# Preparation of the gated delta rule: TensorE convolves two of four batches, inverse lengths laid out by place in the block, the small solve ordered by source column, picks of k issued first

## The reference, cut to what matters

```python
xn = _rmsnorm(x, norm1_w)
xc = silu(_causal_depthwise_conv(xn, conv_w, conv_b))     # K = 4 taps per channel, causal
q = _l2norm((xc @ wq).reshape(b, t, H, HD))               # 16 heads of 8
k = _l2norm((xc @ wk).reshape(b, t, H, HD))
v = (xc @ wv).reshape(b, t, H, HD)
beta = sigmoid(xc @ wb)
alpha = sigmoid(xc @ wa + 4.0)
def step(S, inp):                                         # one token
    q_, k_, v_, b_, a_ = inp
    S = a_[..., None, None] * S
    pred = einsum('bhkv,bhk->bhv', S, k_)
    S = S + k_[..., :, None] * (b_[..., None] * (v_ - pred))[..., None, :]
    return (S, einsum('bhkv,bhk->bhv', S, q_))
```

## Time and profile before

| what | value |
|---|---|
| median of 3 runs | 1909.59 us (1905.56 to 1911.18) |
| the profiled execution, whole | 1912.84 us |
| its span, first to last instruction | 1911.0 us |
| granted TensorE clock, mean | 0.944 |

### The profile page before, as it was taken

The page is one execution under the profiler, slowest core; times in us unless marked ns, Lnnn a source line. Parts: engine busy times, 40 slices in busy tenths (PEclk is TensorE's granted clock), DMA queues, the critical chain, the costliest instruction groups (busy, mean ns, idle before and its releaser), DMA issues.

```text
span 1911.0 us, 24918 instructions
## 1 busy us (share of the span) xinstructions
PE 1671.2 (87%) x8058; PEld 740.8 (39%) x8058; DVE 1307.9 (68%) x3081; ACT 954.3 (50%) x2056; POOL 297.9 (16%) x460
## 2 busy tenths in 40 slices
PE   6789999999999989999799678445897899979998
PEld 2245545544544432222244221222433454534443
DVE  7477767767767767887564689999566777733333
ACT  2555655646645516676434447333244465653333
POOL 0000000000001022111278000000000222104443
PEclk9999999999999989999999889677798899989999
DMA  4000000000000120230000000000100433000000
GB/s 186 1 1 1 1 1 1 1 1 1 1 1 23 50 75 18 59 110 2 1 0 0 1 0 1 1 1 1 66 0 25 122 74 74 3 1 1 1 0 22
DMA packets 19807, 44.37 MB, mean 23 GB/s; under 512 B 3872, under 2 KB 13024, under 8 KB 18912
## 3 DMA queue, kind: packets, MB, share of 16 engines
q1 hardware_dynamic: 19200, 42.39, 7.4%
q10 hardware_dynamic: 480, 0.39, 0.1%
HBM read 32.74 MB, written 9.44 MB: 22 GB/s over the span
## 4 chain that ended last, share of the span: by engine, by line
PE 72%; DVE 18%; ACT 5%; issue 4%; DMA 1%; POOL 0%; ACTq 0%; POOLq 0%; SPq 0%; DVEq 0%
PE ps L569 8%; PE ps L535 7%; PE ps L547 6%; PE ps L1018 5%; PE ps L1056 5%; PE ps L968 5%; PE ps L504 4%; PE ps L1462 3%; PE ps L1463 3%; PE ps L1351 3%; PE ps L1362 3%; PE ps L1470 3%; DVE arena L1801 2%; PE ps L524 2%; PE ps L578 2%
## 5 line engine op out<-in xcount | busy, mean ns | idle before, releaser
L1173 DVE TENSOR_REDUCE stat<-ps 128x1 f32<-128x512 f32 (+3 forms) x512 | 278.7, 582 | 84.6 <-PE ps L968 41.3
L1104 ACT ACTIVATE arena<-ps 128x512 f32<-128x512 f32 (+3 forms) x512 | 246.3, 515 | 150.1 <-PE ps L1056 81.7
L681 ACT ACTIVATE arena<-ps,stat 128x544 f32<-128x544 f32 x256 | 180.4, 709 | 226.0 <-DVE stat L723 226.0
L723 DVE TENSOR_REDUCE stat<-ps 128x1 f32<-128x544 f32 x256 | 173.6, 720 | 144.8 <-PE ps L535 144.0
L1056 PE MATMUL ps<-arena 75*128 75x512 bf16 (+1 forms) x480 | 163.0, 344 | 9.7 <-ACT arena L1104 7.4
L968 PE MATMUL ps<-arena 72*128 72x128 bf16 (+1 forms) x480 | 163.0, 348 | 8.1 <-DVE stat L1173 7.9
L569 PE MATMUL ps<-arena 128*64 128x512 f32 (+1 forms) x640 | 159.7, 611 | 6.3 <-DVE arena L743 5.5
L535 PE MATMUL ps<-arena 64*128 64x272 f32 x1024 | 153.1, 417 | 12.1 <-ACT arena L681 10.4
L689 ACT COPY arena<-ps 128x512 f32<-128x512 f32 x256 | 137.2, 593 | 16.7 <-PE ps L547 16.7
L547 PEld LDWEIGHTS ps<-wA_sb,arena 128*128 128x128 f32 x1024 | 115.1, 142 | 68.7 <-issue 67.9
L547 PE MATMUL ps<-wA_sb,arena 128*128 128x128 f32 x1024 | 140.0, 280 | 0.0
(11 more groups left out here) (352 smaller groups left out, 2822.3 us busy)
## 6 DMA issues: line engine op xcount, KB each, us to landing
arena<-b_parts SPq DMA_DIRECT2D x180, 96.0 KB
b_parts<-arena SPq DMA_DIRECT2D x64, 128.0 KB, 1.8
reg<-wM_dram SPq DMA_DIRECT2D x1, 3072.0 KB, 9.9
reg<-wB_dram SPq DMA_DIRECT2D x1, 2048.0 KB, 12.7
reg<-wM_dram SPq DMA_DIRECT2D x1, 2048.0 KB, 16.7
reg<-wD_dram SPq DMA_DIRECT2D x1, 1817.0 KB, 10.1
wF_sb<-wF_dram SPq DMA_DIRECT2D x1, 1476.0 KB, 19.9
reg<-b_parts SPq DMA_DIRECT2D x12, 96.0 KB
```

Of the source, the lines that this page charges most:

```text
L681: e.activation(prob_of(P, r).rearrange("p (a k) -> p a k", a=2), score_banks(r), ACT.Exp, bias=x_neg[:, at_:at_ + 1], accum_out=x_sums[:, ...
L723: e.tensor_reduce(x_neg[:, n % 4:n % 4 + 1], score_banks(r), AX.XY, ALU.max, negate=True).then_inc(sem("max_done"), 1)
L1104: e.activation(p_t[:, m % 8, q0:T], ps[:, S1 + m % S2, q0:T], ACT.Exp).then_inc(exp_done, 1)
L1173: e.tensor_reduce(nm[:, G % 2, u // 4, u % 4:u % 4 + 1], ps[:, step % S1, 0:keys(u)], AX.X, ALU.max, negate=True).then_inc(max_done, 1)
```

## The change

Four things are rewritten, all in the preparation:

1. Batches 0 and 1 are convolved by TensorE, as four products each with diagonal matrices (`conv_diag`) that add up in banks 4 and 5; Silu reads the bank. POOL makes the four matrices and the zero columns. DVE convolves batches 2 and 3 only. Projections with `g_wa` start batch by batch, and alpha is made batch by batch.
2. The inverse lengths are written by place (`split_i(r)`), so that DVE reads them in planes.
3. The solve goes by source column: one multiply and one subtract take place j out of all later places at once (3, 2 and 1 planes). The six dots go to banks 0 to 5 in the order that this needs, and the solve waits for all of them.
4. `g_ke` is made right behind `g_k`. Gamma and five picks of `g_ke` are issued ahead of the dots, three behind them. `g_pq[0]` is made ahead of the solve and not behind it.

In the diff below the renaming of three semaphores of the first layer (to `padded`, `convolved`, `diag_made`) is left out.

```diff
...
             g_alpha, g_beta = hist_flat[:, 0:BL * M], hist_flat[:, BL * M:2 * BL * M]
-            g_z, g_tmp = terms_flat[:, 0:BL * M], terms_flat[:, BL * M:BL * M + M]
+            g_z, g_tmp = terms_flat[:, 0:BL * M], terms_flat[:, BL * M:BL * M + 3 * M]
             g_pk, k_sq = y_flat[:, 0:6 * M], y_flat[:, 6 * M:10 * M]
...
             r_k, r_q = g_q, qk[:, 0:B * T]
+            conv_diag = qk[:, 9 * M:10 * M].rearrange("p (k n) -> p k n", k=CTAPS)
+            assert CTAPS * D == M
             g_w, g_u, g_ke = (reg2[:, a * B * T:(a + 1) * B * T] for a in range(3))
...
             PK0 = (None, 0, 3, 5)
+            DOT0 = (0, 3, 5)
+            PEB = 2
+            KE_FIRST = 5
             GAMMA, KE, WW, UU, QK, GQ = 0, 1, 9, 17, 21, 31
             PICKS = 39
-            READY = {x: n_ + 1 for n_, x in enumerate(("gamma", "ke", "gq", "w", "u", "q0", "q1", "q2", "q3"))}
+            READY = {x: n_ + 1 for n_, x in enumerate(("gamma", "ke", "gq", "q0", "w", "u", "q1", "q2", "q3"))}
+
+            def by_m(x, n_):
+                return x[:, 0:n_ * M].rearrange("p (i m) -> p i m", i=n_)
 
...
                 e.wait_ge(sem("load_wD"), 16)
-                e.wait_ge(sem("b4_xc"), 1)
+                e.wait_ge(sem("diag_made"), TAPS + CTAPS)
+                e.wait_ge(sem("padded"), 2)
 
...
                     e.matmul(ps[:, bank, :], wt[w], x_aux[:, b, :], start=True, stop=True).then_inc(sem("b4_proj"), 1)
+                for b in range(PEB):
+                    e.wait_ge(*n4.done(b))
+                    for k in range(CTAPS):
+                        i = e.matmul(ps[:, 4 + b, :], conv_diag[:, k, :], xp[:, b, k:k + T], start=(k == 0),
+                                     stop=(k == CTAPS - 1))
+                    i.then_inc(sem("convolved"), 1)
                 for b in range(B):
+                    e.wait_ge(sem("b4_xc"), min(b, PEB) + 1)
                     proj("g_wa", b, b)
...
                              stop=True).then_inc(sem("b4_sum"), 1)
-                e.wait_ge(sem("b4_dve_read"), 2)
-                e.wait_ge(sem("b4_ln"), 2 * B)
-                for s_ in range(1, BL):
-                    e.wait_ge(sem("b4_prod"), s_)
-                    for x in range(PK0[s_], PK0[s_] + BL - s_):
-                        e.matmul(ps[:, x, :], wt["head_one"], g_pk[:, x * M:x * M + M], start=True,
-                                 stop=True).then_inc(sem("b4_dot"), 1)
-
                 def pick(g, matrix, source):
...
                 e.wait_ge(sem("b4_ready"), READY["ke"])
+                e.wait_ge(sem("b4_ln"), 2 * B)
                 pick(GAMMA, pick_k[0], lambda b: split_i(g_gamma)[:, BL - 1, b, :])
                 for d in range(HD):
+                    if d == KE_FIRST:
+                        e.wait_ge(sem("b4_dve_read"), 2)
+                        for s_ in range(1, BL):
+                            e.wait_ge(sem("b4_prod"), s_)
+                            for j in range(BL - s_):
+                                x = PK0[s_] + j
+                                e.matmul(ps[:, DOT0[j] + s_ - 1, :], wt["head_one"], g_pk[:, x * M:x * M + M],
+                                         start=True, stop=True).then_inc(sem("b4_dot"), 1)
                     pick(KE + d, pick_k[d], whole(g_ke))
...
             def b4_act(e):
+                for b in range(PEB):
+                    e.wait_ge(sem("convolved"), PB + b + 1)
+                    e.activation(x_aux[:, b, :], ps[:, 4 + b, :], ACT.Silu, bias=v("conv_b")).then_inc(sem("b4_xc"), 1)
                 e.wait_ge(sem("b4_conv"), CTAPS)
-                e.activation(x_aux[:, :, :], x_aux[:, :, :], ACT.Silu, bias=v("conv_b")).then_inc(sem("b4_xc"), 1)
-                e.wait_ge(sem("b4_proj"), B)
-                e.activation(split_i(g_alpha), tokens_by_i(ps[:, 0:B, :]), ACT.Sigmoid,
-                             bias=v("four")).then_inc(sem("b4_act_read"), 1)
+                e.activation(x_aux[:, PEB:, :], x_aux[:, PEB:, :], ACT.Silu, bias=v("conv_b")).then_inc(sem("b4_xc"), 1)
+                for b in range(B):
+                    e.wait_ge(sem("b4_proj"), b + 1)
+                    i = e.activation(split_i(g_alpha)[:, :, b, :], tokens_by_i(ps[:, b:b + 1, :])[:, :, 0, :], ACT.Sigmoid,
+                                     bias=v("four"))
+                i.then_inc(sem("b4_act_read"), 1)
                 e.wait_ge(sem("b4_proj"), 2 * B)
...
                     for b in range(B):
-                        x, done = r[:, b * T:b * T + T], n_ * B + b + 1
+                        x, done = split_i(r)[:, :, b, :], n_ * B + b + 1
                         e.wait_ge(sem("b4_sum"), done)
-                        e.activation(x, ps[:, 4 + b, :], ACT.Ln, bias=v("eps6")).then_inc(sem("b4_ln"), 1)
+                        e.activation(x, tokens_by_i(ps[:, 4 + b:5 + b, :])[:, :, 0, :], ACT.Ln,
+                                     bias=v("eps6")).then_inc(sem("b4_ln"), 1)
                         e.wait_ge(sem("b4_ln"), done)
...
             def b4_dve(e):
-                link(e, e.memset(xp[:, :, 0:PADW], 0.0))
-                for b in range(B):
+                e.wait_ge(sem("padded"), 2)
+                for b in range(PEB, B):
                     e.wait_ge(*n4.done(b))
+                own = x_aux[:, PEB:, :]
                 for k in range(CTAPS):
                     if k == 0:
-                        i = e.tensor_scalar(x_aux[:, :, :], xp[:, :, 0:T], v("conv_w"), None, ALU.mult)
+                        i = e.tensor_scalar(own, xp[:, PEB:, 0:T], v("conv_w"), None, ALU.mult)
                     else:
                         e.wait_ge(sem("b4_conv"), k)
-                        i = e.scalar_tensor_tensor(out=x_aux[:, :, :], in0=xp[:, :, k:k + T], scalar=v("conv_w", k),
-                                                   in1=x_aux[:, :, :], op0=ALU.mult, op1=ALU.add)
+                        i = e.scalar_tensor_tensor(out=own, in0=xp[:, PEB:, k:k + T], scalar=v("conv_w", k),
+                                                   in1=own, op0=ALU.mult, op1=ALU.add)
                     i.then_inc(sem("b4_conv"), 1)
...
                     e.tensor_tensor(split_i(g_k)[:, :, b, :], tokens_by_i(ps[:, b:b + 1, :])[:, :, 0, :],
-                                    tokens_by_i(r_k[:, b * T:b * T + T].unsqueeze(1))[:, :, 0, :],
-                                    ALU.mult).then_inc(sem("b4_khat"), 1)
+                                    split_i(r_k)[:, :, b, :], ALU.mult).then_inc(sem("b4_khat"), 1)
+                e.wait_ge(sem("b4_khat"), B)
+                e.wait_ge(sem("b4_ready"), READY["gamma"])
+                e.tensor_tensor(g_ke, g_k, g_to_end, ALU.mult).then_inc(sem("b4_ready"), 1)
                 e.wait_ge(sem("b4_act_read"), 2)
-                e.wait_ge(sem("b4_khat"), B)
                 link(e, e.tensor_tensor(g_z, g_k, g_beta, ALU.mult))
...
                 e.tensor_tensor(split_i(g_q), tokens_by_i(ps[:, 0:B, :]),
-                                tokens_by_i(r_q.rearrange("p (b t) -> p b t", b=B)), ALU.mult).then_inc(sem("b4_dve_read"), 1)
-                e.tensor_tensor(g_ke, g_k, g_to_end, ALU.mult).then_inc(sem("b4_ready"), 1)
+                                split_i(r_q), ALU.mult).then_inc(sem("b4_dve_read"), 1)
                 e.wait_ge(sem("b4_dve_read"), 2)
+                e.wait_ge(sem("b4_ready"), READY["ke"])
                 e.tensor_tensor(g_gq, g_q, g_gamma, ALU.mult).then_inc(sem("b4_ready"), 1)
+                e.tensor_tensor(g_pq[0], g_q, g_k, ALU.mult).then_inc(sem("b4_ready"), 1)
                 e.wait_ge(sem("b4_prod"), BL - 1)
+                e.wait_ge(sem("b4_dot"), len(DOT0) * (len(DOT0) + 1) // 2)
                 for x in (g_w, g_u):
                     x_ = by_i(x)
-                    for i in range(1, BL):
-                        for s_ in range(1, i + 1):
-                            pair = PK0[s_] + i - s_
-                            e.wait_ge(sem("b4_dot"), pair + 1)
-                            link(e, e.tensor_tensor(g_tmp, ps[:, pair, :], x_[:, i - s_, :], ALU.mult))
-                            o = e.tensor_tensor(x_[:, i, :], x_[:, i, :], g_tmp, ALU.subtract)
-                            if i == s_ == BL - 1:
-                                o.then_inc(sem("b4_ready"), 1)
-                                e.wait_ge(sem("b4_ready"), READY["w" if x is g_w else "u"])
-                            else:
-                                link(e, o)
-                for s_ in range(BL):
+                    for j in range(BL - 1):
+                        n_ = BL - 1 - j
+                        link(e, e.tensor_tensor(by_m(g_tmp, n_), ps[:, DOT0[j]:DOT0[j] + n_, :],
+                                                x_[:, j, :].unsqueeze(1).to_broadcast([128, n_, M]), ALU.mult))
+                        o = e.tensor_tensor(x_[:, j + 1:, :], x_[:, j + 1:, :], by_m(g_tmp, n_), ALU.subtract)
+                        if n_ == 1:
+                            o.then_inc(sem("b4_ready"), 1)
```

(31 more changed lines are left out.)

## The result

The changed kernel has a median of 1901.17 us over 8 runs (1892.79 to 1910.70), the kernel before 1909.98 beside it; the ratio is 0.9953, 95% interval 0.9930 to 0.9976. So it is faster by 0.5%, some 9 us. The forecast was 1900.1 and faster by over 0.3%.

A forecast was written before the change was run, and what follows sets the result against it. Two strands, picks on TensorE and ACT and DVE's work, end together before the scan, so both must shorten. Terms sum to -11.0 us, less 1.5 for the clock: 9.5 us less, median 1900.1, range 1895 to 1905.

The forecast's parts named there:

- Convolution, -7.75: From the last norm product to beta: with TensorE convolving two batches, beta starts 7.75 us earlier, partly through clock.
- Lengths by place, -0.4 and -1.45: Scaling of k and q on DVE: SBUF operand in planes saves 0.4 us on k's last batch, 1.45 on q.
- the SBUF rival: Scaling of k and q: SBUF steps are free, PSUM's cost, so 7.65 us less, 1901.9; chance 0.04.
- `g_ke` forward, +2.3, and dots, +1.0: On DVE, `g_ke` ahead of `g_z` adds 2.3 us; waiting for six dots starts the solve 1.0 later behind `g_q`.
- Solve, -2.35: DVE's solve by source column: 15.05 us instead of 17.4, so 2.35 less.
- The rival rate of `g_q`: Solve's multiplies run at the slower rate of `g_q`: +4.4 us, 5.1 less in all, 1904.5; chance 0.06.
- `g_pq[0]`, -2.33: This DVE product moves from behind the solve into the wait for the dots, saving 2.33 us.
- The sum on VectorE, -11.0: All terms of the preparation together, with the clock never falling: 11.0 us less.
- Clock, +1.5: Two new TensorE gaps, before q's sums and before picks of `g_w`, slow the products behind them: 1.5 us lost.
- the rival's 11.0: Clock holds in both new TensorE gaps, so the full 11.0 us is gained, 1898.6; chance 0.30.
- The other rivals: Convolution slow at lower clock: 2.7 us less, 1906.9, chance 0.04; scan's start at lower clock: slower, 1921, chance 0.03.
- What would show it: Listed signs; right: scan's first step 9 to 11 us earlier; wrong: DVE wait over 3 us, memset-to-last-copy over 1 us.

The follow-up runs named there:

- e1: Changed kernel with all four batches convolved by VectorE again; stretch from last norm product to scan 83.01 us against 75.20, ratio to the kernel before 0.9988.
- e3: Changed kernel with inverse lengths stored by token again and scaled with the old reads; stretch from last norm product to scan 77.62 us against 75.20, one run.
- e7: Changed kernel with the solve by target column again, 24 instructions each waiting for its own dot; stretch 75.52 us against 75.20, one run.
- e8: Changed kernel plus beta by batch, dots in solve order with each step awaiting its own, three picks first; stretch 72.37 us, ratio to before 0.9927.
- e0: Changed kernel once more, nothing edited; stretch 75.20 us, rest of span 1823.9 us, ratio to the kernel before 0.9952.
- e5: Changed kernel with three and not five picks of g_ke ahead of the dots; stretch 75.93 us against 75.20, one run.
- e6: Changed kernel with no pick of g_ke ahead of the dots, only gamma; stretch 76.52 us against 75.20, one run.

## Why the prediction was right, point by point

- *Convolution, -7.75.* Measured 7.75 from the last norm product to beta, 7.8 by e1. Right, with the clock's share in it: 8.97 against 7.24 us for the projections.
- *Lengths by place, -0.4 and -1.45.* In the profile 0.4 and 1.47; e3 gives 2.1 on VectorE and 2.4 with the picks. The row of `g_u` was the right one to go by, and the SBUF rival fell.
- *`g_ke` forward, +2.3, and dots, +1.0.* `g_u` ended 9.1 us earlier than before with the norm 3.1 earlier, so 6.0 in all, where 5.85 was the sum; the solve started 5.58 us behind `g_q`, where I had 5.35.
- *Solve, -2.35.* It takes 15.11 us, 2.29 less. The rival rate of `g_q` didn't show: multiplies over three banks with a repeated plane take 1.76, 1.22 and 0.69. As a term for VectorE's work it was right; as a gain of the stretch by itself it was too large. Put back alone (e7) it costs 0.3, since its gain is partly spent in the wait for all dots and behind the picks.
- *`g_pq[0]`, -2.33.* It is made in the wait for the dots, as said; not tried by itself.
- *The sum on VectorE, -11.0.* From the last norm product to VectorE's memset it was 84.08 us and is 73.24: 10.84 less. Each term came within 0.3 of its size, so the mechanism and not only the total held.
- *Clock, +1.5.* Half wrong. I put 1.1 on the gap ahead of the sums of q and 0.4 on that ahead of the picks. The first did nothing in the profiles of the changed kernel (3.70 us for four sums each time); with the clock lost there, as in e1, e3, e7 and e8, the solve began 0.4 us later in e1 and no later in e3, e7 and e8. The second came each time and cost more, 0.8 between VectorE's end and the last copy. But before the change the copy already ended 0.4 behind VectorE, which the sum left out, so only 0.4 of the 0.8 is lost against before. Against the 10.84 the clock took 0.4, where I had 1.5. So the stretch fell by 10.45, between the forecast's 9.5 and the rival's 11.0.
- *The other rivals.* The convolution's products took 0.86 us each and came forward, and the first 27 us of the scan had clock 1.00 as before, so neither of those two showed.
- *What would show it.* A wait of 1.05 us ahead of the solve, 0.8 between memset and last copy, first step 10.45 us earlier: as listed. "The same distance to the end from there" didn't hold: this distance was 739.2 us in the first profile and 746.0 in e0, and was never a constant to a few us. The median came 8.8 us lower, within its uncertainty of the 10.45. That it lies 1.1 us from the forecast is partly luck: the interval of the ratio spans 0.46%, some 9 us.

## What to carry to other kernels

Follow a preparation to where its strands meet: work moved off a strand counts only until another strand, here the picks, ends last. An idle engine with a clock to lose is worth filling even with work that another engine would do in the same time, and a reordering should be judged by every gap that it moves, since e5 closed one and opened another. Where a kernel's later part has gaps behind which the clock is sometimes kept and sometimes lost, judge a small edit by its own stretch in a profile and time it in many runs; single times of one program differed here by 20 us.

## What the runs showed of the hardware

- VectorE reading an SBUF f32 operand in steps of 4 columns: 3.75 to 3.97 us for 2048 columns, against 2.28 with the operand in planes; the same steps in PSUM cost nothing.
- Gaps on TensorE in the preparation and what followed: 1.72 us, clock kept (e8); 2.18, kept (e5); 2.71, lost (e5); 3.11, lost (e7); 3.29, lost (e8); 3.75, lost (e3); 4.43 to 4.45, lost each time; 5.82, lost (e6). At 3.36 to 3.37 us the same code went either way: ahead of the sums of q it was kept in six of eight profiles and lost in e1 and e7; behind the scan the clock over the next 5 us was 1.00 in seven of fourteen and 0.50 to 0.70 in the others.
- In the changed kernel's first eight executions the mean granted clock went from 0.943 to 0.955 and the time from 1910.70 to 1892.79 us.
- At clock 1.00 eight wide products whose moving operand (the one that streams through) has steps of 512 columns in SBUF take 14.22 us in the chain of the changed kernel (1.78 each), twice the 0.86 of products on contiguous columns:

```profile
1162.35 14.22 PE ps L1653 x16
```
